# Second attention: one full 128-row product in front of the tiles of each slot from the thirteenth to the fifty-third

## What is computed

```python
x = x + _L0_attn_b_ref(_layernorm(x, axis=-1), L0_attn_b_qkv_w, L0_attn_b_qkv_b, L0_attn_b_proj_w, L0_attn_b_proj_b)
...
attn = jnp.einsum('abhqd,abhkd->abhqk', q, k) * scale
attn = jax.nn.softmax(attn, axis=-1)
out = jnp.einsum('abhqk,bhkd->abhqd', attn, v)
...
out = out @ proj_w.T + proj_b
```

## Time and profile before

| what | value |
|---|---|
| time, median of 3 runs | 1106.29 us (1105.43 to 1106.92) |
| time of the profiled execution | 1103.96 us |
| its span, first to last instruction | 1102.2 us |
| mean granted TensorE clock over the span | 0.868 of full |
| PE busy | 980.6 us, 89% |
| DVE busy | 975.5 us, 89% |
| ACT busy | 667.2 us, 61% |

### The profile page before, as it was taken

The page is one execution under the profiler, slowest core; times in us unless marked ns, Lnnn a source line. Parts: engine busy times, 40 slices in busy tenths (PEclk is TensorE's granted clock), DMA queues, the critical chain, the costliest instruction groups (busy, mean ns, idle before and its releaser), DMA issues. The chain is left out here.

```text
span 1102.2 us, 17415 instructions
## 1 busy us (share of the span) xinstructions
PE 980.6 (89%) x5387; PEld 700.9 (64%) x5387; DVE 975.5 (89%) x1482; ACT 667.2 (61%) x779; POOL 360.7 (33%) x226
## 2 busy tenths in 40 slices
PE   6767888888369999999999899999879999999997
PEld 4533444444247788888888555555568888888886
DVE  7799999999978999999999787988688999999997
ACT  4779999999634544544554553666545454455444
POOL 2054666666701333333341120100113333334330
PEclk9855555555659999999999998999989999999999
DMA  2000000000107755555550000111138555655531
GB/s 58 1 1 1 1 1 1 1 1 1 51 10 179 190 152 155 149 148 158 150 145 18 1 1 1 17 19 21 35 95 209 154 150 149 158 153 144 159 83 38
DMA packets 50710, 86.93 MB, mean 79 GB/s; under 512 B 20092, under 2 KB 33404, under 8 KB 50556
## 3 DMA queue, kind: packets, MB, share of 16 engines
q1 hardware_dynamic: 50664, 86.34, 30.2%
HBM read 83.33 MB, written 2.98 MB: 78 GB/s over the span
## 5 line engine op out<-in xcount | busy, mean ns | idle before, releaser
L1490 ACT ACTIVATE sg<-ps 128x512 f32<-128x512 f32 x264 | 156.8, 594 | 265.8 <-PE ps L513 264.2
L513 PE MATMUL ps<-xh,whi 128*128 128x512 f32 x528 | 206.3, 391 | 1.3 <-ACT b L1318 1.3
L513 PE MATMUL ps<-xl,whi 128*128 128x512 f32 x528 | 205.9, 390 | 0.0
L513 PE MATMUL ps<-xh,wlo 128*128 128x512 f32 x528 | 205.8, 390 | 0.0
L2300 DVE TENSOR_TENSOR hf<-sg,ps 128x512 f32<-128x512 f32 x264 | 170.2, 684 | 30.8 <-DVE hl L2307 24.3
L1674 POOL CAST whi<-wraw 128x384 fp32r<-128x384 f32 x66 | 67.8, 1027 | 380.1 <-PE ps L513 287.7
L1614 POOL TENSOR_TENSOR rr<-xr,rr 128x2048 f32<-128x2048 f32 x32 | 144.7, 4551 | 130.2 <-ACT rr L1293 76.5
L2307 DVE TENSOR_TENSOR hl<-hf,hh 128x1024 fp32r<-128x1024 f32 x132 | 179.1, 1357 | 0.5 <-DVE hf L2300 0.5
L2312 DVE TENSOR_TENSOR hf<-hf,cbc 128x1024 f32<-128x1024 f32 x128 | 157.6, 1231 | 14.5 <-DVE hf L2300 2.0
L1517 ACT ACTIVATE hh<-hf 128x1024 fp32r<-128x1024 f32 x132 | 139.2, 1054 | 4.9 <-DVE hf L2312 4.9
L1676 POOL TENSOR_TENSOR wlo<-wraw,whi 128x384 fp32r<-128x384 f32 x66 | 116.9, 1771 | 5.3
(11 more groups left out here) (273 smaller groups left out, 1543.3 us busy)
## 6 DMA issues: line engine op xcount, KB each, us to landing
cbc<-routing_coefficients SPq DMA_DIRECT2D x256, 256.0 KB, 3.8
wraw<-in_wexp_dram SPq DMA_DIRECT2D x66, 192.0 KB, 2.7
X<-in_x_dram SPq DMA_DIRECT2D x4, 256.0 KB, 4.8
routing_coefficients<-cT SPq DMA_DIRECT2D x8, 128.0 KB, 2.4
out_dram<-X SPq DMA_DIRECT2D x4, 256.0 KB, 2.9
heads_by_row<-o_all SPq DMA_DIRECT2D x12, 72.0 KB
b_rows<-heads_by_row SPq DMA_DIRECT2D x12, 72.0 KB, 2.7
rope_in<-in_consts_dram SPq DMA_DIRECT2D x1, 512.0 KB, 3.4
```

The source lines that it names most:

```text
L513: return pe.matmul(o, l, r, start=start, stop=stop, **kw)
L1490: act.activation(sg[c % 2][:, :], bank(4 + 2 * (c % 2)), ACT.Silu).then_inc(s_sg, 1)
```

## The change

One more branch stands in `b_tiles`. It gives one product to every slot from U = 12 to U = 52 that had none; the six slots of `WAITS_FOR_PATH` keep their three or four, and slots 0 to 11 their two.

```diff
                 if 0 <= U < 12:
                     keep_busy(2 + 2 * (U % 2), 2)
                 elif V in WAITS_FOR_PATH:
                     keep_busy(2 + 2 * (U % 2), WAITS_FOR_PATH[V])
+                elif 0 <= U < 53:
+                    keep_busy(2 + 2 * (U % 2), 1)
                 for i in range(2):
                     if scores and V >= 1:
                         pe.wait_ge(s_mx, 2 * (V - 1) + i + 1)
```

## The result

| | before | after |
|---|---|---|
| median of 18 runs each, on the same chips | 1105.21 us (1100.85 to 1108.35) | 1108.14 us (1104.97 to 1110.43) |
| ratio | | 1.0027, 95% interval 1.0016 to 1.0037 |
| span of the profiled execution | 1102.2 us | 1106.8 us |
| exponential of slot 12 to that of slot 53 | 74.50 us | 77.06 us |

The kernel is slower, by 2.9 us between the medians; the interval gives 1.8 to 4.1 us. Single executions of one kernel lie up to 7.5 us apart, so most of what follows is read from the slots themselves: the time from the exponential of slot 12 to that of slot 53. Slots 0 to 12, which the change leaves alone, took 21.10 us in both profiled executions, and 21.09 to 21.14 in the profiles of all later kernels that keep their products in slots 0 to 11, so as long as the clock stays full this measure is far steadier than the total.

The account below looks back on a forecast made before the run. Neither PE nor DVE was full; a two-slot loop or DVE's work set the pace. The slot terms, 0.28 + 0.63 + 2 x 0.45 + 2 x 0.21 + 5 x 0.11 = 2.8 us, gave 1109.1 us, range 1106.6 to 1111.8.

Parts of the forecast that it names:

- The price: On PE between values and tiles: 0.45 us per product in 18 slots, 0.21 in 17 behind a 128-row step; 11.7 in all.
- The cover: Slots 12 to 52: three quarters of the 11.7 us on PE lie beside DVE's reduces, so 2.8 us pass through.
- slots 12 and 13: 0.28 us together: A (first tiles) of slot 12 waited 0.17 for the reduce, so 0.28 of 0.45 remains.
- 17 to 21: 0.63 us: in slots 18 and 20 the reduce waits for the first tiles, and the two-slot loop gives up its slack.
- the plain ones around 26 and 42: 0.45 us in slot 26 and 0.45 in slots 41 to 43; the reduce of slot 26 waits for PE already.
- 33 and 49: Slots behind the projection: 0.21 us each in full, with DVE waiting 0.89 and 0.88.
- The five groups behind steps of the maxima: Behind 128-row steps (slots 14 to 16, 22 to 24, 29 to 32, 38 to 40, 45 to 48): 0.11 us each.
- Slots with U mod 4 = 3: The values there wait for ACT's copy, 0.26 us late, so 0.26 is free.
- Behind slot 53: Nothing takes the delay up there, so the 2.8 us pass through to the total.
- a single product doesn't pay the change: Plain slots: one product costs 0.21 us instead of 0.45; 1.8 us in all, 1108.1; chance 0.28.
- everything costs more: All slots lose 0.235 us as the delay reaches ACT's copy; up to 8.2 us, 1114.5; chance 0.07.
- The clock: Denser PE might prevent falls of the granted clock; up to 2.3 us back, about 1105.8 with cheap products; chance 0.05.

Follow-up runs that it names:

- the two sets of slots: Changed kernel with products only in 11 slots reckoned covered: slots 74.66 us; only in 8 reckoned uncovered (12, 13, 18, 20, 26, 33, 42, 49): 76.72 us.
- the covered set: Changed kernel with its product only in slots 19, 21, 25, 27, 29, 34, 37, 41, 43, 45, 50: slots 74.66 us against 74.50 before.
- the 1.76 of the plain slots: Changed kernel with products only in the 18 slots where no step of 128 rows stands ahead: slots 76.26 us, 1.76 more than before.
- the best version: Kernel before with two products instead of three or four in slots 28, 35, 36, 44, 51, 52: slots 73.14 us, ratio 0.9976.

## Why the prediction was right

- *The price.* Foretold 0.45 in a plain slot and 0.21 behind a step; measured 0.42 and 0.22. The change back to tiles of 32 rows costs 0.20, at the lower edge of the 0.20 to 0.24 that I had.
- *The cover.* "Only what passes DVE's reduces counts" is shown by the two sets of slots (0.16 for 11 products, 2.22 for 8), foretold as 0.2 and 2.2. The growth came where it was foretold: 0.94 by slot 20 (1.0 foretold), 0.52 more by slot 28 (0.6), 0.30 by slot 36, 0.50 by slot 44 and 0.30 by slot 52 (the terms of the sum give 0.32, 0.56 and 0.32).
- *Where the 0.2 us between 2.8 and 2.56 lie.* By the starts of the values, before and after, the terms came out as 0.28 for slots 12 and 13 (0.28 foretold), 0.60 for 17 to 21 (0.63), 0.44 and 0.42 for the plain ones around 26 and 42 (0.45 each), 0.25 and 0.24 for 33 and 49 (0.21 each). The five groups behind steps of the maxima (14 to 16, 22 to 24 and so on) came out as 0.06 or 0.07 each instead of 0.11, 0.33 together instead of 0.55. Nearly the whole difference is this term: more of the 0.22 is covered there than the 0.10 that I took off.
- *Slots with U mod 4 = 3.* The wait for ACT's copy vanished in slots 19, 27 and 43, as the slack there implied, and the covered set, with three such slots (19, 27, 43), stayed nearly free.
- *Behind slot 53* all 2.55 us passed through to slot 63.
- *The rivals.* That a single product doesn't pay the change fell with the 0.42 and with the 1.76 of the plain slots (0.9 by that rival). That everything costs more fell with the cover. The clock did not move in the slots, so its rival as put (a gain) did not occur. But I gave it 0.05 by the row of 1.00 alone, without asking what held it there. The runs show that products of 128 rows hold it, those that were there already. Had there been none in the six slots, single products would have been a gain: without any the slots took 81.11 us, with one in each of the 41 75.40.
- *The range* was for the median; 1108.14 lies in it, 1.0 us below the forecast, mostly because the median of before, with more runs, is 1.1 us lower (1105.21 instead of 1106.29). The difference between the kernels, 2.9 us, was foretold as 2.8. That the absolute figure came so near is partly luck. I took the median to lie 2.3 us above the profiled execution in both kernels. It lies 0.5 below it in the changed one: the profiled execution was foretold as 1106.8 and took 1108.67, most of it the 1.6 us that coincide with the lower clock near the end.

## What to carry to other kernels

Price an added instruction by the wait it stands in, slot by slot: where a consumer waits for this engine now, it costs most of its time (2.2 of 3.0 us here), and where the engine itself waits next, it costs almost nothing (0.16 of 4.6) until that slack is used up; a second one then costs more than the first. A product that fills TensorE between products of another division of the array costs the change as well as its columns, so put it beside work of its own kind (0.22 instead of 0.42 here). And a clock row of 1.00 doesn't say that the filler (products that nobody reads) is needless or that more is needed: take the filler away in steps and watch the clock, as the best version here came from fewer products and not from more.

## What the runs showed of the hardware that was not expected

TensorE's full clock was not kept by its being busy as such. With 32-row products in 41 slots the profile has it busy for 38.1 of 39 us, and then the clock fell from 2.4 to 1.2 GHz (windows of 1.00, then 0.54). With products of the same columns and 128 rows in the same slots, 38.3 of 39 us busy and a wait of 0.26 us ahead of slot 36 (0.27 in the other), the windows stayed at 1.00. Without either it fell at about the same place (0.56). The Trainium skill, "TensorE: Matmul & The Clock Gate", What's actually happening, ties the clock to how busy TensorE has been; these two runs do not fit that taken alone. What it is about the 32-row products that loses the clock was not separated further.

A product put between two kinds of work can cost a change of the array's division beside its own time. From values (128*32) to a product (128*128) it takes 0.57 us, as from values to tiles (32*128), and from the product to the tiles 0.42, which is 0.20 more than its own 0.22. The Trainium skill, "TensorEngine Tiling (Array Packing)", Tiling Modes, speaks of a drain at each change of mode; the trace agrees for the change from product to tiles. What the change behind the values costs it doesn't show, because something of another division follows the values in every slot.
